# Values projected token by token and shifted by a DMA, in a hybrid of two attentions and an FFN

## The chip, the cores and the metric

The program runs on one core of a Trainium2 chip. Its engines are TensorE (PE), VectorE (DVE), ScalarE (ACT), GpSimd (POOL) and SyncE (SP, which only issues DMAs here). Each takes its instructions in the order in which they are written, and engines wait for each other through semaphores. The metric is the device time of one execution in microseconds, lower is better.

## The reference

Four layers with residual sums on x of 4 batches x 2048 tokens x 256 channels, float32: causal attention A, an FFN with token shift, attention B, and the FFN again. Each takes a layer norm of x.

```python
x = x + attn_a(layernorm(x), q_proj, k_proj, v_proj, o_proj)          # 16 heads of 16
x = x + ffn(layernorm(x), W_r, W_k, W_v, mu_r, mu_k)
x = x + attn_b(layernorm(x), W_k, W_v, W_c, leaky_key_beta, key_scale, v_coef, val_scale)
x = x + ffn(layernorm(x), ...)                                        # the same weights
```

The change lies in the keys and values of attention B:

```python
k = (x @ W_k.T)  # by head; then a decaying sum over earlier tokens
k = einsum('hij,bhjd->bhid', exp(-(i - j) * beta_h) for j <= i, k)
k = k / (norm(k) + 1e-10) * exp(min(10 * key_scale, KEY_SCALE_MAX))
v = (x @ W_v.T)
v_shift = concatenate([v[:, :, 1:], zeros])
v = (1 - v_coef) * v_shift + v_coef * v       # v_coef: one number per head
v = v / (norm(v) + 1e-10) * exp(10 * val_scale)
q = k[:, :, 1:]                               # queries are the keys one token on
```

Queries are the keys one token later, so the kernel keeps values one place back as well: at place n it mixes the value of token n-1 (times `v_coef`) and the value of token n (times `1 - v_coef`).

## The kernel before

There are eight attentions (A and B, each for four batches), and each has four groups of four heads: 32 instances. An instance is a row of 68 slots. In a slot PE computes the scores of a group of two 128x512 blocks (three slots ahead), ACT takes their exponential into `probs`, POOL masks the blocks on the diagonal (`mask`, the last five groups of each of the four query chunks), and PE multiplies earlier `probs` with `v_st`. The query chunks end with slots 4, 17, 38 and 67; after each, `take` on DVE transposes the sums out of PSUM (`o_blk`, which sets the semaphore `s_o`), divides them (`o_norm`), and for every second head group transposes them to `o_out`, which SP stores to memory. Two banks of PSUM (6 and 7) alternate between the query chunks; the one not in use serves all side work.

The side work is cut into jobs of one chunk of 512 tokens. P jobs normalize x and project queries, keys and values of attention A. M jobs project the attention's output (`o0`, `o1`), add it to x, normalize, turn `xn` (`t0`, `t1`), and run the FFN (`k`, `r`, `f`). MA jobs (16, four batches x four chunks) go on with attention B: normalize again, turn (`bt0`, `bt1`), project keys (`bk0`, `bk1`) and values (`bv0`, `bv1`). Keys run through a scan on DVE and a transposition in blocks (`k_blk`), POOL squares them (`buf_a`). Values are projected channel by channel into `vT` (copied by ACT), so that the shift by one token is a shift along the row; POOL weights them (`buf_u`), DVE mixes them, PE turns them to tokens (`vt0`, `vt1`, line 981), ACT copies them to `buf_v`, POOL squares them into `buf_k`. Then DVE sums both kinds of squares and computes the inverse lengths of keys and values in one row of operations on 128 columns (line 1389 on), gives `v_fac` to POOL and scales the keys.

The order is written out by hand: the tables `T_P`, `T_M`, `T_B` and `T_END` hold a slot offset for each step, and a step stands on its engine at the job's start plus this offset; in one slot the main work comes first, then the jobs in their order. M jobs start four slots before an instance (`FRONT`). Each side part waits with `free_bank` until the part before it in its bank is emptied and until the bank's query chunk has been taken:

```python
if part.before:
    pe.wait_ge(s_side[part.bank], part.before)
if part.seg > 0:
    pe.wait_ge(s_o, part.seg)
```

Three slots before each instance all engines read flags that tell whether a head needs its row maxima; DVE, SP and PE branch there. Four heads of the run are flagged.

Of the kernel before, what the change touches and what calls it, by code (L numbers as in the profile page):

```python
# [105 lines left out]
class Job:  # L106
# [4 lines left out]
    def __init__(self, kind, b, c, att, t0, off=None):  # L111
# [8 lines left out]
T_P0 = {"load": -10, "ln": 0, "t0": 6, "t1": 8, "u0": 14, "u1": 16, "u2": 18, "u3": 20, "v0": 22, "v1": 24, "n": 28,  # L120
# [3 lines left out]
T_M = {"load": -10, "o0": 0, "o1": 2, "ln": 3, "t0": 12, "t1": 14, "diff": 13, "shift": 16, "k0": 18, "k1": 20, "r0": 26,  # L124
       "r1": 28, "f0": 30, "f1": 32, "out": 34}
# [6 lines left out]
PE_PARTS["MA"] = PE_PARTS["MB"] + ("bt0", "bt1", "bk0", "bk1", "bv0", "bv1", "vt0", "vt1")  # L132
# [3 lines left out]
def job_list():  # L136
# [15 lines left out]
    jobs += [Job("MB", 3, c, 7, start(7, 3) + (16, 37, 58, 82)[c], T_END) for c in range(NCH)]  # L152
# [84 lines left out]
JOB = {(j.kind, j.b, j.c): j for j in JOBS}  # L237

# [17 lines left out]
def hybrid_kernel(nc, t, out):  # L256
    with ExitStack() as ctx:
# [31 lines left out]
        vT = sb("vT", [P, KT, CH + 1])  # L289
# [117 lines left out]
        def _(sp):  # L407
# [68 lines left out]
            def load_o(j):  # L476
# [91 lines left out]
            def main(slot):  # L568
# [6 lines left out]
                if 0 <= n < NI and i in LAST_OF and n % 2:  # L575
# [970 lines left out]
```

## Time and profile before

| | |
|---|---|
| Median of 3 runs (lowest, highest) | 3010.07 us (3009.12, 3013.25) |
| The profiled execution | 3010.78 us, span 3009.1 us |
| PE busy | 2862.4 us, 95% |
| ACT busy | 2232.7 us, 74% |
| DVE busy | 1472.8 us, 49% |
| POOL busy | 817.1 us, 27% |
| Mean granted clock of PE | 0.976 |

"Busy" is the time in which an engine executes something; waiting and issuing are not in it. Each row of a timeline is one or several like instructions, with the idle time of the engine just before it in brackets and what ended it. PE's records of a float32 matmul come in pairs, so 32 records are 16 matmuls.

### The profile page before, as it was taken

The numbers are of one execution on the slowest core, as the hardware profiler recorded it, in microseconds if no ns is written. First come the engines' busy times: TensorE is split into PE (matmuls) and PEld (weight loads), VectorE is DVE, ScalarE is ACT, GpSimd is POOL, SyncE is SP. The second block draws the span as 40 slices with busy tenths as digits, with TensorE's granted clock in tenths as the row PEclk, the third lists the DMA queues.
The fourth block names the chain that finished last, engine by engine and source line by source line (L and its number), as shares of the span: only waits on it lengthen the run. The fifth ranks groups of instructions, "written<-read, shape, count | busy, mean of one in ns | idle before, by whom it ended". The sixth has DMA issues, their size and how long they took to land.

```text
span 3009.1 us, 99722 instructions
## 1 busy us (share of the span) xinstructions
PE 2862.4 (95%) x42984; PEld 1302.0 (43%) x42984; DVE 1472.8 (49%) x3579; ACT 2232.7 (74%) x2487; POOL 817.1 (27%) x1246
## 2 busy tenths in 40 slices
PE   6999999999999899998999999999999989999897
PEld 3444444444444344444444444444444434444343
DVE  5322346565556654445344434555665656523544
ACT  2799978787787478784788878778787856788472
POOL 4222223332323222221222222232333322322111
PEclk9999999999999899998999999999999999999898
DMA  5322312222222123222322223222222221222111
GB/s 136 106 83 81 95 53 78 70 73 67 81 71 60 52 67 103 81 76 67 95 81 74 82 89 94 64 78 68 63 75 71 73 66 52 72 72 85 41 62 41
DMA packets 229828, 225.34 MB, mean 75 GB/s; under 512 B 33221, under 2 KB 212933, under 8 KB 229320
## 3 DMA queue, kind: packets, MB, share of 16 engines
q1 hardware_dynamic: 228504, 217.47, 25.3%
q8 instruction: 356, 5.83, 0.8%
q14 instruction: 152, 1.25, 0.1%
q10 hardware_dynamic: 816, 0.79, 0.1%
HBM read 146.80 MB, written 71.32 MB: 72 GB/s over the span
## 4 chain that ended last, share of the span: by engine, by line
PE 72%; DVE 16%; issue 6%; ACT 4%; POOL 1%; SPq 0%; DVEq 0%; DMA 0%; ACTq 0%
PE ps L872 46%; PE ps L1103 23%; ACT probs L828 4%; DVE pmax L1434 3%; PE ps L884 3%; DVE xn L1198 2%; DVE nw_y L1180 1%; DVE nw_u L1178 1%; DVE ln_st L1186 1%; DVE nw_u L1176 1%; DVE x_buf L1315 1%; DVE o_blk L1493 1%; DVE k_blk L1413 1%; DVE nw_v L1389 1%; POOL buf_k L703 0%
## 5 line engine op out<-in xcount | busy, mean ns | idle before, releaser
L828 ACT ACTIVATE probs<-ps 128x1024 f32<-128x1024 f32 x2176 | 2083.1, 1059 | 477.7 <-PE ps L872 474.5
L872 PE MATMUL ps<-q_st,k_st 99*32 99x512 bf16 (+3 forms) x20480 | 1237.4, 349 | 5.0 <-issue 2.4
L1103 PE MATMUL ps<-probs,v_st 128*17 128x512 f32 (+3 forms) x10240 | 1160.7, 532 | 22.4 <-POOL probs L731 13.1
L872 PEld LDWEIGHTS ps<-q_st,k_st 99*32 99x32 bf16 x20480 | 567.0, 96 | 775.7 <-issue 449.6
L731 POOL TENSOR_SCALAR_AFFINE_SELECT probs<-probs 128x256 f32<-128x256 f32 (+1 forms) x896 | 433.4, 501 | 1138.7 <-ACT probs L828 1120.1
L1103 PEld LDWEIGHTS ps<-probs,v_st 128*17 128x17 f32 x10240 | 291.9, 98 | 272.2 <-issue 59.1
L872 PE MATMUL ps<-xT,wT 128*32 128x512 f32 x2048 | 242.6, 594 | 0.0
L1493 DVE STREAM_TRANSPOSE o_blk<-ps 128x512 f32<-128x512 f32 x128 | 91.0, 711 | 269.2 <-PE ps L1103 268.9
L657 POOL TENSOR_TENSOR parts<-rest,parts 128x512 bf16<-128x512 f32 x96 | 120.9, 1260 | 316.7 <-DVE parts L1221 316.7
L1348 DVE SCALAR_TENSOR_TENSOR buf_v<-buf_v,ps 128x512 f32<-128x512 f32 x64 | 44.0, 687 | 272.9 <-PE ps L872 272.9
L1315 DVE TENSOR_TENSOR x_buf<-x_buf,ps 128x512 f32<-128x512 f32 x64 | 43.8, 684 | 217.6 <-PE ps L872 207.2
L872 PE MATMUL ps<-wT,o_in 128*32 128x256 f32 x2048 | 124.3, 380 | 14.5 <-issue 14.5
L872 PE MATMUL ps<-buf_k,wT 128*32 128x512 f32 x1024 | 124.7, 609 | 8.2 <-DVE buf_k L1335 8.0
L872 PEld LDWEIGHTS ps<-xT,wT 128*32 128x32 f32 x2048 | 65.1, 109 | 139.8 <-issue 136.1
L872 PE MATMUL ps<-wT,buf_u 128*32 128x256 f32 x2048 | 121.9, 379 | 1.6 <-issue 1.6
L872 PE MATMUL ps<-wT,buf_a 128*32 128x256 f32 x2048 | 121.6, 379 | 0.6 <-issue 0.5
L884 PE MATMUL ps<-ident,xn 128*128 128x128 f32 x512 | 85.8, 293 | 34.7 <-DVE xn L1198 24.5
L792 ACT ACTIVATE buf_u<-ps 128x512 f32<-128x512 f32 x64 | 38.2, 597 | 99.9 <-PE ps L872 99.9
L884 PEld LDWEIGHTS ps<-ident,xn 128*128 128x128 f32 x512 | 55.8, 145 | 125.1 <-DVE xn L1198 63.1
L1216 DVE TENSOR_TENSOR rest<-ps,parts 128x512 f32<-128x512 f32 x64 | 44.1, 690 | 133.5 <-ACT parts L778 133.5
L681 POOL TENSOR_TENSOR buf_a<-xf 128x512 f32<-128x512 f32 x32 | 33.2, 1037 | 270.3 <-DVE xf L1204 255.5
L1198 DVE TENSOR_SCALAR xn<-x_buf,ln_mv,nw_y 128x256 f32<-128x256 f32 x256 | 99.3, 450 | 2.3
(140 smaller groups left out, 2148.9 us busy)
## 6 DMA issues: line engine op xcount, KB each, us to landing
part_a<-parts SPq DMA_DIRECT2D x192, 128.0 KB
x_buf<-in_L_attn_a_X SPq DMA_DIRECT2D x32, 512.0 KB, 4.6
q_st<-part_a SPq DMA_DIRECT2D x128, 128.0 KB
o_chan<-o_out SPq DMA_DIRECT2D x64, 256.0 KB, 2.4
o_in<-o_chan SPq DMA_DIRECT2D x64, 256.0 KB, 4.6
q_st<-part_b SPq DMA_DIRECT2D x128, 128.0 KB
k_st<-part_a SPq DMA_DIRECT2D x64, 192.0 KB, 2.9
part_b<-parts SPq DMA_DIRECT2D x96, 128.0 KB
```

What stands on the lines that cost most here:

```text
L657: pool.tensor_tensor(parts[:, u % NPARTS, 2, :], rest[:, u % 2, :], parts[:, u % NPARTS, 1, :], ALU.subtract).then_inc(s_low, 1)
L731: last = pool.affine_select(out=o, in_=o, compare_op=ALU.is_ge, fill=0.0, base=0, pattern=[[0, o.shape[1]], [1, P]], channel_multiplier=-1)
L828: nc.scalar.activation(probs[:, g % NP_BUF, :], ps[:, bk:bk + 2, :].rearrange("p a n -> p (a n)"), ACT.Exp, scale=SCALE[ATT[g // (NHG * NG ...
L872: last = pe.matmul(o[c:c + 32], kt[:, c:c + 32], q, **how)
L884: last = pe.transpose(ps[:, part.bank, tb * P:(tb + 1) * P], src[:, tb, kt * P:(kt + 1) * P], ident[:, :])
L1103: last = pe.matmul(ps[32 * j:32 * j + VW, bank, q0:q0 + w], v_st[:, k % 2, kb, hg * HG + j, :], p, start=(kb == 0), stop=(kb >= TB * qc), ...
L1198: last = nc.vector.tensor_scalar(xn[:, tb, :], x[:, tb, :], ln_mv[:, tb, 0:1], nw_y[:, tb:tb + 1], ALU.subtract, ALU.mult)
L1216: nc.vector.tensor_tensor(left, src, high, ALU.subtract).then_inc(s_side[part.bank], 1)
L1315: nc.vector.tensor_tensor(half(x, i), half(x, i), ps[:, part.bank, :], ALU.add).then_inc(s_side[part.bank], 1)
L1348: nc.vector.scalar_tensor_tensor(half(gate, i), half(gate, i), 1.0, ps[:, part.bank, :], ALU.add, ALU.mult).then_inc(s_side[part.bank], 1)
L1434: nc.vector.tensor_reduce(pmax[:, 1 if b0 else 0, qb:qb + 1], src, AX_X, ALU.max).then_inc(s_mx["used"], 1)
L1493: nc.vector.transpose(o_blk[:, sg % 2, :], ps[:, 6 + sg % 2, :]).then_inc(s_o, 1)
```

## The change

Values of attention B are now projected token by token (`project_tokens`) straight into the layout in which they are used; ACT copies them to `v_raw`. SP shifts them by one token with three DMAs within SBUF: 127 partitions of `v_raw` to the next partition of `v_before` (the memory of `buf_k`), the last partition to the first of the next block, and the very last token to `v_edge` for the next chunk; POOL places the edge. POOL weights `v_raw` with `v_rest`, DVE mixes per head with factors that are spread over the elements of a head (four operations for two), POOL squares. `vt0` and `vt1` are gone. The lengths are computed in two rows of operations on 64 columns, of keys (`klen`) and of values (`vlen`), at two places.

The tables move further steps: `o0` and `o1` of all M jobs stand two slots earlier, with their loads; the normalization of the first batch's chunks stands five slots earlier, with a wait on PE's turn of the chunk before; at the start x of the second chunk is loaded only when the first has landed. The last four jobs start 6 to 13 slots earlier, and the last output chunk's second half goes from DVE into `o_in` without a store and a load.

```diff
-T_P0 = {"load": -10, "ln": 0, "t0": 6, "t1": 8, ...}
+T_P0 = {"load": -16, "ln": -5, "t0": 6, "t1": 8, ...}
-T_M = {"load": -10, "o0": 0, "o1": 2, "ln": 3, "t0": 12, ...}
-T_B = {"lnb": 32, "bt0": 40, "bt1": 46, "bk0": 48, "bk1": 50, "bv0": 52, "bv1": 54, "w": 55, "u": 57, "vt0": 59, "vt1": 61,
-       "len": 63, "keys": 69, "split": 91, "vb": 70, "low": 94, "store": 98}
+T_M = {"load": -12, "o0": -2, "o1": 0, "ln": 3, "t0": 12, ...}
+T_B = {"lnb": 32, "bt0": 40, "bt1": 46, "bk0": 48, "bk1": 50, "bv0": 52, "bv1": 54, "w": 55, "vsh": 56, "u": 61, "vsq": 63,
+       "klen": 55, "vlen": 73, "split": 91, "vb": 82, "low": 94, "store": 98}
+T_LAST = {**T_END, "o_load": -4}
...
-    jobs += [Job("MB", 3, c, 7, start(7, 3) + (16, 37, 58, 82)[c], T_END) for c in range(NCH)]
+    jobs += [Job("MB", 3, c, 7, start(7, 3) + (10, 24, 45, 69)[c], {**T_LAST, "load": -4} if c == 2 else T_LAST) for c in range(NCH)]
...  SP
+                yield j.t0 + j.off["vsh"]
+                for i in range(2):
+                    sp.wait_ge(*emptied(j.at[f"bv{i}"]))
+                sp.dma_start(v_before[1:P], v_raw[0:P - 1]).then_inc(s_vsh, 16)
+                sp.dma_start(v_before[0:1, 1:TB, :], v_raw[P - 1:P, 0:TB - 1, :]).then_inc(s_vsh, 16)
+                sp.wait_ge(s_edge, j.at["ma"] + 1)
+                sp.dma_start(v_edge[:, :], v_raw[P - 1:P, TB - 1, :]).then_inc(s_vsh, 16)
...
-            for c in range(2):
-                load_x(JOB["P", 0, c])
+            load_x(JOB["P", 0, 0])
+            sp.wait_ge(s_x[0], 16)
+            load_x(JOB["P", 0, 1])
...  POOL
-                    pool.tensor_scalar(buf_u[:, m, :], vT[:, m, 1:CH + 1], v_rest[:, m:m + 1], None,
+                    pool.tensor_tensor(by_head(half_of(buf_u, i)), by_head(half_of(v_raw, i)), per_head(v_rest),
                                        ALU.mult).then_inc(s_w1, 1)
...
+                    pool.wait_ge(s_u, 2 * n + i + 1)
+                    pool.tensor_tensor(half_of(buf_k, i), half_of(buf_v, i), half_of(buf_v, i), ALU.mult).then_inc(s_vsq, 1)
...  PE
+                        if j is LAST_JOB:
+                            pe.wait_ge(s_o_in, 32 * f + 16)
+                            pe.wait_ge(s_ot, len(ATT) * KT * NCH)
...
+                    if at == j.off[f"bv{i}"]:
+                        project_tokens(j.at[f"bv{i}"], BV, i, src)
...  DVE
+            def inverse_lengths(at):
+                step(nc.vector.tensor_scalar(nw_v[:, at], nw_v[:, at], 1.0e-30, None, ALU.max))
+                settle()
+                rsqrt(at)
+                step(nc.vector.tensor_tensor(nw_u[:, at], nw_v[:, at], nw_y[:, at], ALU.mult))
+                settle()
+                step(nc.vector.tensor_scalar(nw_u[:, at], nw_u[:, at], NORM_EPS, None, ALU.add))
+                settle()
+                step(nc.vector.reciprocal(nw_y[:, at], nw_u[:, at]))
+                settle()
...
+                yield j.t0 + j.off["u"]
+                dve.wait_ge(s_edge, n + 1)
+                dve.wait_ge(s_vsh, 48 * (n + 1))
+                for i in range(2):
+                    step(nc.vector.tensor_tensor(by_head(half_of(buf_v, i)), by_head(half_of(v_before, i)), per_head(v_coef),
+                                                 ALU.mult))
+                    settle()
+                    dve.wait_ge(s_w1, 2 * n + i + 1)
+                    nc.vector.tensor_tensor(half_of(buf_v, i), half_of(buf_v, i), half_of(buf_u, i), ALU.add).then_inc(s_u, 1)
+                yield j.t0 + j.off["vlen"]
                 dve.wait_ge(s_vsq, 2 * (j.at["ma"] + 1))
+                step(sums(buf_k, of_values))
+                settle()
+                inverse_lengths(of_values)
...
+                    if sg == NI * NCH - 1:
+                        dve.wait_ge(s_part, JOBS[-2].at["o1"].n + 1)
+                        dst = o_in[:, KT - 1, :]
```

DVE at the start of a new instance, before: after the normalization of the job that has just begun (`xn`) comes `take` of the new instance's first query chunk.

```order
L1178 SCALAR_TENSOR_TENSOR nw_u<-nw_u,nw_v 128x4
L1180 SCALAR_TENSOR_TENSOR nw_y<-nw_u,nw_y 128x4
L1198 TENSOR_SCALAR xn<-x_buf,ln_mv,nw_y 128x256 x4
L1493 STREAM_TRANSPOSE o_blk<-ps 128x512
L1496 TENSOR_SCALAR den<-o_blk 128x16
```

The same place of the changed kernel (nine more operations of the inverse root on 128x64 stand where rows are left out):

```order
L1236 TENSOR_SCALAR xn<-x_buf,ln_mv,nw_y 128x256 x4
L1208 TENSOR_REDUCE nw_v<-buf_k 128x64
L1211 TENSOR_SCALAR nw_v<-nw_v 128x64
L1195 TENSOR_SCALAR nw_y<-nw_v 128x64
L1197 TENSOR_SCALAR nw_y<-nw_y 128x64
...
L1214 TENSOR_TENSOR nw_u<-nw_v,nw_y 128x64
L1216 TENSOR_SCALAR nw_u<-nw_u 128x64
L1218 RECIPROCAL nw_y<-nw_u 128x64
L1443 TENSOR_TENSOR v_fac<-nw_y,v_scale 128x64
L1525 STREAM_TRANSPOSE o_blk<-ps 128x512
```

The lengths of the previous job's values have moved from before the change of instance to between `xn` and `o_blk`; this is so in all 16 jobs.

PE at the change of instance, before (`wT,o_in` are the parts `o0` and `o1`, `TENSOR_LOAD` and the branch read the flags):

```order
L1103 MATMUL ps<-probs,v_st 17x512 x4
L872 MATMUL ps<-wT,o_in 32x256 x16
L1142 TENSOR_LOAD flags_a
L1143 COMPARE_AND_BRANCH
L872 MATMUL ps<-q_st,k_st 32x512 x16
L1103 MATMUL ps<-probs,v_st 17x384 x4
L1103 MATMUL ps<-probs,v_st 17x128 x4
L872 MATMUL ps<-wT,o_in 32x256 x16
```

And in the changed kernel:

```order
L1127 MATMUL ps<-probs,v_st 17x512 x4
L901 MATMUL ps<-wT,o_in 32x256 x16
L901 MATMUL ps<-q_st,k_st 32x384 x4
L901 MATMUL ps<-q_st,k_st 32x128 x4
...
L901 MATMUL ps<-q_st,k_st 32x256 x16
L1127 MATMUL ps<-probs,v_st 17x512 x4
L901 MATMUL ps<-wT,o_in 32x256 x16
L1166 TENSOR_LOAD flags_a
L1167 COMPARE_AND_BRANCH
```

Both output projections now stand ahead of the branch.

SP in the last quarter of an MA job's instance, before, with the loads of the next job behind the keys:

```order
L511 DMA k_st<-part_a 48x4x512
L511 DMA k_st<-part_a 32x4x512
L511 DMA k_st<-part_a 16x4x512
L435 DMA x_buf<-in_L_attn_a_X 128x4x256
L483 DMA o_in<-o_chan 128x512 x2
```

And in the changed kernel:

```order
L539 DMA k_st<-part_a 16x4x512
L486 DMA buf_k<-v_raw 127x1024
L487 DMA buf_k<-v_raw 1x16x48
L489 DMA v_edge<-v_raw 1x16x16
L452 DMA x_buf<-in_L_attn_a_X 128x4x256
L511 DMA o_in<-o_chan 128x512 x2
```

The three DMAs of the shift stand ahead of the next job's loads.

## Rows read from the trace of the kernel before

**Rows 1.** The page's busy times: us (share of the span) xinstructions.

```profile
PE 2862.4 (95%) x42984; PEld 1302.0 (43%) x42984; DVE 1472.8 (49%) x3579; ACT 2232.7 (74%) x2487; POOL 817.1 (27%) x1246
```

**Rows 2.** Waits of PE: engine, line <- releaser: us in total, times, longest.

```profile
PE ps L1103 <- POOL probs L731: 13.1, 9, 2.5
...
PE ps L884 <- DVE o_blk L1493: 10.1, 14, 1.2
```

**Rows 3.** Groups of PE by form: busy us, mean ns | idle before.

```profile
L872 PE MATMUL ps<-xT,wT 128*32 128x512 f32 x2048 | 242.6, 594 | 0.0
...
L872 PE MATMUL ps<-wT,o_in 128*32 128x256 f32 x2048 | 124.3, 380 | 14.5 <-issue 14.5
...
L872 PE MATMUL ps<-wT,xT 128*32 128x256 f32 x1024 | 64.3, 391 | 0.5 <-DVE rest L1216 0.5
...
L981 PE MATMUL ps<-ident,buf_u 128*128 128x128 f32 x128 | 21.0, 287 | 0.0
```

**Rows 4.** Timeline, a change of head group: start, us, engine, [idle before <-releaser].

```profile
556.33 1.04 PE L872 MATMUL ps<-q_st,k_st 99*32 99x512 bf16 x16
...
558.63 0.67 DVE L1315 TENSOR_TENSOR x_buf<-x_buf,ps 128x512 f32<-128x512 f32 x1
...
559.40 1.93 PE L872 MATMUL ps<-wT,o_in 128*32 128x256 f32 x32 [1.17 <-issue]
...
561.13 0.65 PE L872 MATMUL ps<-q_st,k_st 99*32 99x384 bf16 x16
...
563.37 1.38 DVE L1413 TENSOR_TENSOR k_blk<-k_blk,nw_v 128x1024 f32<-128x1024 f32 x1 [3.28 <-issue]
...
565.58 1.05 PE L1103 MATMUL ps<-probs,v_st 128*17 128x512 f32 x8 [2.49 <-POOL probs L731]
```

**Rows 5.** Timeline, a change of head group without lengths of values.

```profile
1295.86 0.65 PE L1103 MATMUL ps<-probs,v_st 128*17 128x256 f32 x8
...
1297.15 0.70 DVE L1493 STREAM_TRANSPOSE o_blk<-ps 128x512 f32<-128x512 f32 x1
...
1299.48 0.34 DVE L1192 BATCH_NORM_AGGREGATE ln_mv<-ln_st 128x2 f32<-128x6 f32 x4
...
1303.53 0.71 DVE L1493 STREAM_TRANSPOSE o_blk<-ps 128x512 f32<-128x512 f32 x1
...
1304.43 0.66 PE L884 MATMUL ps<-ident,xn 128*128 128x128 f32 x4
```

**Rows 6.** Groups of DVE by form.

```profile
L1178 DVE SCALAR_TENSOR_TENSOR nw_u<-nw_u,nw_v 128x4 f32<-128x4 f32 x192 | 33.9, 176 | 6.6
...
L1389 DVE TENSOR_REDUCE nw_v<-buf_k 128x64 f32<-128x1024 f32 x16 | 19.5, 1220 | 76.7 <-POOL buf_k L703 76.7
...
L1178 DVE SCALAR_TENSOR_TENSOR nw_u<-nw_u,nw_v 128x128 f32<-128x128 f32 x48 | 18.6, 388 | 1.6
...
L1399 DVE RECIPROCAL nw_y<-nw_u 128x128 f32<-128x128 f32 x16 | 15.2, 953 | 0.6
```

**Rows 7.** Waits of all engines: DVE before the keys' scaling.

```profile
DVE k_blk L1413 <- issue: 22.1, 7, 3.3
```

**Rows 8.** Timeline of the tail, PE.

```profile
2957.04 2.59 PE L1103 MATMUL ps<-probs,v_st 128*17 128x384 f32 x24 [1.96 <-issue]
...
2966.02 6.05 PE L872 MATMUL ps<-buf_k,wT 128*32 128x512 f32 x32 [4.78 <-DVE buf_k L1335]
...
2975.35 1.90 PE L872 MATMUL ps<-wT,o_in 128*32 128x256 f32 x32
...
2991.79 5.12 PE L872 MATMUL ps<-buf_k,wT 128*32 128x512 f32 x32 [3.24 <-DVE buf_k L1335]
```

**Rows 9.** Windows: us, busy by engine, then the granted clock of PE.

```profile
742.03:745.44 3.41, 3.41 (x40) 1.75 (x36) 3.03 (x16) 1.94 (x2) 0.00 (x0) 0.50 0.19 70
```

**Rows 10.** Timeline of the head.

```profile
36.46 0.66 PE L884 MATMUL ps<-ident,xn 128*128 128x128 f32 x4 [2.60 <-DVE xn L1198]
```

**Rows 11.** DMA issues of the page: KB each, us to landing.

```profile
x_buf<-in_L_attn_a_X SPq DMA_DIRECT2D x32, 512.0 KB, 4.6
```

More of the change, by code:

```diff
@@ L481, in load_o @@
                 for m in range(KT):
+                    if j is LAST_JOB and m == KT - 1:
+                        continue
                     sp.wait_ge(s_o_out[j.c % 2], 16 * ((k * KT + m) * (NCH // 2) + j.c // 2 + 1))
@@ L678, in m_job @@
                 if any(i.kind == "MA" for i in earlier):
-                    pool.wait_ge(s_vfac, [i for i in earlier if i.kind == "MA"][-1].at["ma"] + 1)
+                    pool.wait_ge(s_ksum, [i for i in earlier if i.kind == "MA"][-1].at["ma"] + 1)
                 pool.wait_ge(*emptied(j.at["t0"]))
@@ L850, in params @@
                 for kt in range(KT):
-                    pe.matmul(ps[:, 0, 2 * kt:2 * kt + 2], sel_ch[:, kt * P:(kt + 1) * P], head_col[:, 0:2],
-                              start=True, stop=True)
+                    pe.matmul(ps[:, 0, kt:kt + 1], sel_ch[:, kt * P:(kt + 1) * P], head_col[:, 0:1], start=True, stop=True)
                 for i in range(4):
@@ L855, in params @@
                 pe.matmul(ps[:, 1, 0:H], ones_row[:, :], head_row[:, :], start=True, stop=True)
+                pe.matmul(ps[:, 1, H:2 * H], ones_row[:, :], coef_row[:, :], start=True, stop=True)
                 pe.matmul(ps[0:1, 2, 0:H], head_col[:, 2:3], ident[0:H, 0:H], start=True, stop=True).then_inc(s_hp_ps, 1)
@@ L966, in m_job @@
                         turn(j.at[f"bt{kt}"], xn, kt)
[L967 to L983 removed]
+                for i in range(2):
+                    if at in (j.off[f"bk{i}"], j.off[f"bv{i}"]):
+                        for kt in range(KT):
+                            pe.wait_ge(*emptied(j.at[f"bt{kt}"]))
+                    if at == j.off[f"bk{i}"]:
+                        project_channels(j.at[f"bk{i}"], BK, i, src)
+                    if at == j.off[f"bv{i}"]:
+                        project_tokens(j.at[f"bv{i}"], BV, i, src)
             def row_maxima(n, j):
@@ L1251, in p_job @@
             def p_job(j):
-                yield j.t0
+                yield j.t0 + j.off["ln"]
+                if j.b == 0 and j.c:
+                    dve.wait_ge(s_part, JOB["P", 0, j.c - 1].at["t1"].n + 1)
                 x_there(j)
@@ L1372, in m_job @@
                     nc.vector.transpose(k_blk[:, m, :], kT[:, m, :]).then_inc(s_kblk, 1)
-                yield j.t0 + j.off["u"]
-                for m in range(KT):
-                    dve.wait_ge(s_w1, 2 * j.at["ma"] + m + 1)
-                    nc.vector.scalar_tensor_tensor(buf_u[:, m, :], vT[:, m, 0:CH], v_coef[:, m:m + 1], buf_u[:, m, :],
-                                                   ALU.mult, ALU.add).then_inc(s_u, 1)
-                dve.wait_ge(s_u, 2 * (j.at["ma"] + 1))
-                if j.c < NCH - 1:
-                    nc.vector.tensor_copy(vT[:, :, 0:1], vT[:, :, CH:CH + 1]).then_inc(s_vlast, 1)
-                else:
-                    nc.vector.memset(vT[:, :, 0:1], 0.0).then_inc(s_vlast, 1)
@@ L1391, in m_job @@
-                settle()
-                step(nc.vector.tensor_scalar(nw_v[:, :], nw_v[:, :], 1.0e-30, None, ALU.max))
-                settle()
-                rsqrt(P)
-                step(nc.vector.tensor_tensor(nw_u[:, :], nw_v[:, :], nw_y[:, :], ALU.mult))
-                settle()
-                step(nc.vector.tensor_scalar(nw_u[:, :], nw_u[:, :], NORM_EPS, None, ALU.add))
-                settle()
-                step(nc.vector.reciprocal(nw_y[:, :], nw_u[:, :]))
-                settle()
```

134 lines of the change are left out of this document (67 added, 67 removed).

## The prediction

> **What bounds the kernel now.** I read the page's busy times first: PE is busy for 95% of the span, ACT and DVE for 74% and 49% [rows 1]. So time is what PE computes plus what PE stands idle, 147 us in all. Next PE's own waits, to see who makes it idle: at most of the head-group changes it waits a short time for DVE's `o_blk` and for POOL's masks [rows 2], and the second `o_in` projection of a job is preceded by idle time as well, 14.5 us over the run, labelled "issue" [rows 3]. The timeline at one such change shows that the label misleads. `x_buf` is added by DVE at 558.63, only after a long row of small operations on lengths, and the next `o_in` matmul starts 0.1 us after that add has ended: both use one bank of PSUM, so PE had waited for DVE. Then DVE stands 3.28 us at the branches on the flags, adds the second half, and PE's products with `v_st`, which need the same bank, start at 565.58 after 2.49 us [rows 4]. So DVE's order around a change of head group decides PE's idle time, and there the change must be weighed.
>
> **Transposes and projection.** 16 jobs (four batches by four chunks) give up 8 PE transposes each: the row with `buf_u` has 128, 21.0 us [rows 3]. Their values are projected token by token: 64 records of 256 columns in a job for 32 of 512. By the rows 64 x 62.8 ns = 4.02 us for 32 x 118.5 ns = 3.79 us; by the `o_in` row (60.7 ns) 3.88 us. That is +1.5 to +3.6 us in all, and I take +2.5. PE is the bound wherever this lies, so the sum is -18.5 us. ACT loses two copies in a job; it is not the bound.
>
> **The earlier `o_in` projections.** They move two slots forward, and the second one now stands ahead of the branch on PE, and its add ahead of the flag branches on DVE. DVE's small operations on keys are now done some ten slots before, on values after the change of group. So the waits of that timeline should go: 14.5 us before `o_in` [rows 3], and 10.1 and 13.1 us from the two wait rows [rows 2], 37.7 us; I take -37 (-34 to -41).
>
> **The chain of the values' lengths.** This is the step that speaks against the change. In the order of DVE it now stands behind the `xn` of the next job and directly ahead of the first `o_blk` of the new head group, in all 16 jobs. PE's first transposes of `xn` (slot 8) wait for that `o_blk`, because it empties their bank, and everything on PE queues behind them. The same place without lengths of values, where PE waits for nothing, gives the cover [rows 5]. PE's last products of the old group end at 1296.51, its transposes start at 1304.43: 7.92 us. DVE needs 2.33 us from its first `o_blk` to the normalization (0.71 less where the head group is even and `o_out` isn't written), 4.05 us to the second `o_blk`, and 0.74 us until that bank is free. With 0.1 us to start that is 7.2 us, so 0.7 us of cover. Now the chain: a sum of 1.22 us, 14 operations on 64 columns, a reciprocal and `v_fac`. No row has them at 64 columns. At 4 columns one takes 0.18 us, at 128 0.39 us [rows 6], each with 0.03 us to the next; the 128 figure includes operations beside a busy POOL, which is idle here between its masks, so I take 0.25 us with the gap. 1.22 + 3.5 + 0.55 (reciprocal, 0.95 at 128) + 0.35 = 5.7 us; the bounds are 4.7 us (all as at 4 columns) and 8.0 us (all as at 128). PE's stall is then 5.7 - 0.7 = 5.0 us, 4.3 us at even groups, 4.7 us on average. DVE also has to pass the flag branches first: seven times of 16 these cost it 3.3 us [rows 7]. After the second add and statistics (1.4 us) that is 4.7 us, and PE has 3.0 us of scores and products from there to the end of the group (556.33 to 558.23, and 1.1 us from 561.13), so DVE comes 1.7 us late in such a case, 0.8 us on average. 16 x 5.5 us = +88 us (+59 with the chain at 4.7 us and no branch time, +125 at 8.0 us).
>
> **TensorE's clock.** After an idle time of 4.78 us the next 32 records took 6.05 us, after 3.24 us 5.12 us [rows 8], for 3.79 us at full clock [rows 3]: 2.3 and 1.3 us lost, at the lower of its two levels (1.2 for 2.4 GHz). I take 1.8 us for each of 16 stalls, +29 us, less three stretches of 1.7 us that the present short waits bring (one is the row of 742.03 [rows 9]; the others are alike): +24 us. The row of 565.58 had 2.49 us of idle time before it and ran at its full speed (1.05 us for 8 records), so not every short wait costs the clock; at changes of the head group three of the six between 2.1 and 2.7 us did. The Trainium skill, "TensorE: Matmul & The Clock Gate", section "Part 1: The HAM clock gate", calls the throttled state the default, which activity releases. If the busy stretches on both sides are activity enough by that rule, a 5 us stall passes as the one of 2.49 us did, and the sum is the second rival's below; by the two waits of [rows 8] it does not pass, and I follow the rows.
>
> **The shift by DMA.** Its wait adds a risk on DVE: behind it stand the adds of `o_in`. No row shows a transfer within SBUF. The nearest are `x_buf` from memory, 512 KB in 4.6 us [rows 11], and I take 4 us (2.4 to 10). Issued in slot 52, it lands about when DVE has finished the keys' chain (some 8.5 us from slot 51); the mixing (four operations, 3.3 us) ends some 2 us before the first add is due. Cost 0; if the cover goes, each us more is 16 us in the sum. POOL's squares end just before its masks: 0 as well.
>
> **Head and tail.** At the start PE waits three times 2.6 us for `xn` of the next chunk [rows 10]; the normalization now stands ahead of the splits. DVE's own work in a chunk is some 13 us for PE's 12.6, so two thirds of it come back, 6 us. But the parameters, which DVE still awaits first, are now issued only after the first chunk has landed, which costs 1 to 2 us. Together -5 (-8 to +2). In the tail PE's products end at 2959.63, the last `o_in` parts stand behind work of the job before (8 transposes, 32 records of 512 and 64 of 256 columns: 1.3 + 3.8 + 3.9 = 9 us at the rates of [rows 3]), and the first starts at 2975.35 [rows 8]. Now the last half of `o` comes from DVE without memory, some 2.5 us after the products, and those 9 us are moved ahead of them, where PE pays them too. 2975.35 - 2959.63 - 2.5 - 9 = 4 us: -4 (-11 to +2, as the earlier jobs wait more closely for their `o_in`).
>
> **Sum.** -18.5 - 37 + 88 + 24 - 5 - 4 = +47.5 us against the profiled execution of 3010.78 us (span 3009.1 us, and 1.7 us around it), 0.7 us over the median of the three timed ones: 3058, and against the median 3057 us.
>
> **Rivals.** First, the other side: the `o_blk` is not late. If DVE passes normalization and chain within PE's 7.92 us, or PE reaches its transposes later than I think, the 88 and 24 us are gone: -18.5 - 37 - 5 - 4 = -64.5, 2946 us. For it speaks that DVE is busy only 49% of the span; against it that the cover is 0.7 us and the shortest chain is 4.7 us. It decides only from a chain under 0.7 us, or if another row of slots lies between.
> Second, the stalls come but the clock mostly stays: half of them pay 1.7 us, 14 - 5 = +9 in place of 24, 3043 us. For it the 2.49 us case; against it [rows 8].
> Third, the shift lands late, say after 10 us. Then the mixing ends 4 us after the adds are due, POOL's masks and PE behind them: 16 x 4 = +64, 3122 us. Against it: `x_buf` in 4.6 us.
> Fourth, balance: chain 4.7 us and no branch time (+59), clock +17, and the gains at their upper ends (-19.5, -41, -8, -11): -3.5, 3007 us.
> That the change doesn't do what it says I can exclude by the order: no transposes of `buf_u` are left, and three DMAs stand in each job.
>
> **How the numbers follow.** The likeliest case 0.62, its own range 3020 to 3100 (chain 4.7 to 7 us); clock stays 0.14; not late 0.12; late landing 0.07; balance 0.05. The range reaches from the balanced case to most of the high bound of the chain (88 becomes 125: 3094 and the clock above): 3005 to 3110, which leaves out 2946 and the late landing. What can be told from no change is 0.2%, 6 us. Faster by more: the 0.12 and half the balanced case, 0.15; the same 0.03; slower 0.82.
>
> **What would show it.** PE before its first transposes of `xn` in a new head group: idle 4 to 7 us, released by `o_blk`, 16 times. The chain on 64 columns between `xn` and `o_blk`: 5 to 6.5 us. No idle time before the second `o_in`. Half-clock stretches after those transposes. No PE row with `buf_u` transposes, and PE's busy time 18 us less but for the clock's part. The shift lands within 6 us. The forecast is wrong if `o_blk` is there before PE, or if the mixing waits for the DMA into the adds.

## The result and the profile after

The changed kernel takes 3423.3 us (median of 4 runs, 3421.4 to 3426.5) against 3009.8 us: a ratio of 1.1372, 95% interval 1.1353 to 1.1392. It is slower, as forecast, but by 413 us where 47 were forecast. The profiled execution took 3423.03 us, its span is 3421.3 us.

From the page after: busy times [rows 1], then the chain of work that ended last, by engine and by line.

```profile
PE 2913.5 (85%) x43370; PEld 1341.3 (39%) x43370; DVE 1548.4 (45%) x3833; ACT 2215.4 (65%) x2455; POOL 797.8 (23%) x1261
...
PE 63%; DVE 14%; SPq 8%; DMA 7%; issue 5%; ACT 2%; POOL 0%; DVEq 0%; ACTq 0%
PE ps L901 41%; PE ps L1127 19%; DMA o_in<-o_chan 6%; SPq L487 4%; PE ps L913 2%; DVE pmax L1466 2%; SPq L511 2%; DVE xn L1236 2%; ACT probs L857 2%; DVE nw_u L1200 1%; DVE nw_u L1202 1%; DVE o_blk L1525 1%; DVE nw_y L1204 1%; SPq L489 1%; SPq L539 1%
```

PE's busy time rose by 51 us and its idle time from 147 to 508 us. The reader is to see two names that had no part in the profile before: a DMA of `o_in`, and SP's own queue at L487, the second of the three DMAs of the shift. The groups of the page say who waited for what (busy, mean ns | idle before, releaser). The first is the group of `wT,o_in` in [rows 3], the second has the waits for `o_blk` of [rows 2], and the third is DVE's mixing:

```profile
L901 PE MATMUL ps<-wT,o_in 128*32 128x256 f32 x2048 | 153.9, 450 | 310.0 <-DMA o_in<-o_chan 308.0
...
L913 PE MATMUL ps<-ident,xn 128*128 128x128 f32 x512 | 96.0, 318 | 128.4 <-DVE o_blk L1525 108.3
...
L1433 DVE TENSOR_TENSOR buf_v<-buf_k,v_coef 128x512 f32<-128x512 f32 x32 | 22.0, 688 | 359.8 <-DMA v_edge<-v_raw 359.8
```

In each of the 16 jobs PE stands 18.4 to 19.6 us ahead of the first projection of `o_in`, and DVE 22.5 us on average for the shift. The timeline of one job, SP's issues (how long each took) and the two that waited:

```profile
450.56 0.69 SPq L486 DMA_DIRECT2D buf_k<-v_raw  x1
...
451.30 8.25 SPq L487 DMA_DIRECT2D buf_k<-v_raw  x1
...
459.59 0.85 SPq L489 DMA_DIRECT2D v_edge<-v_raw  x1
460.49 0.59 SPq L452 DMA_DIRECT2D x_buf<-in_L_attn_a_X  x1
461.18 6.13 SPq L511 DMA_DIRECT2D o_in<-o_chan  x2
467.35 4.44 SPq L539 DMA_DIRECT2D k_st<-part_a  x3
475.48 0.69 DVE L1433 TENSOR_TENSOR buf_v<-buf_k,v_coef 128x512 f32<-128x512 f32 x1 [22.27 <-DMA v_edge<-v_raw]
...
477.69 3.64 PE L901 MATMUL ps<-wT,o_in 128*32 128x256 f32 x32 [18.56 <-DMA o_in<-o_chan]
```

The shift's first DMA was issued at 450.56 and the data were there at 475.48. The trace has 127 packets of 4096 bytes in this time, one for each row of L486, from 452.00 to 474.49, with a mean of 181 ns: 127 x 181 ns = 23.0 us of packet time in 22.5 us, hardly more than one packet under way at any moment. I read that as one of the 16 DMA engines carrying them all; rows118 and rows124 test it. The packets of `o_in` bear it out: of the 256 of its two DMAs, issued from 461.18 on, 240 had started by 469.83, and the other 16, one in 16, ran from 475.89 to 477.09, behind the shift. The first projection then also ran at the lower level of the clock (the granted clock was 0.50 from 462.24 to 482.72): 3.64 us for the 32 records that took 1.93 us before [rows 4].

The stalls that the prediction spoke of are there as well: the 108.3 us above. DVE's operations around one of them, the last before `o_blk` being those of the lengths, and PE behind:

```profile
493.44 1.39 DVE L1236 TENSOR_SCALAR xn<-x_buf,ln_mv,nw_y 128x256 f32<-128x256 f32 x4
494.74 1.22 DVE L1208 TENSOR_REDUCE nw_v<-buf_k 128x64 f32<-128x1024 f32 x1
...
500.08 0.22 DVE L1443 TENSOR_TENSOR v_fac<-nw_y,v_scale 128x64 f32<-128x64 f32 x1
500.23 0.71 DVE L1525 STREAM_TRANSPOSE o_blk<-ps 128x512 f32<-128x512 f32 x1
...
501.08 1.09 PE L913 MATMUL ps<-ident,xn 128*128 128x128 f32 x4 [4.91 <-DVE o_blk L1525]
```

From 494.74 to 500.23 the chain takes 5.5 us, and PE waits 4.91.

### The profile page after: what moved, and what is told of

It reads as the page before. It is cut to its first block, busy times and chain, and to the rows that moved or that the text cites. A ratio compares the mean times of both kernels' runs of the same rounds, so it can differ in the third digit from the quotient of the medians.

```text
span 3421.3 us, 100825 instructions
## 1 busy us (share of the span) xinstructions
PE 2913.5 (85%) x43370; PEld 1341.3 (39%) x43370; DVE 1548.4 (45%) x3833; ACT 2215.4 (65%) x2455; POOL 797.8 (23%) x1261
## 4 chain that ended last, share of the span: by engine, by line
PE 63%; DVE 14%; SPq 8%; DMA 7%; issue 5%; ACT 2%; POOL 0%; DVEq 0%; ACTq 0%
PE ps L901 41%; PE ps L1127 19%; DMA o_in<-o_chan 6%; SPq L487 4%; PE ps L913 2%; DVE pmax L1466 2%; SPq L511 2%; DVE xn L1236 2%; ACT probs L857 2%; DVE nw_u L1200 1%; DVE nw_u L1202 1%; DVE o_blk L1525 1%; DVE nw_y L1204 1%; SPq L489 1%; SPq L539 1%
## 5 line engine op out<-in xcount | busy, mean ns | idle before, releaser
L901 PE MATMUL ps<-q_st,k_st 99*32 99x512 bf16 (+3 forms) x20480 | 1258.5, 355 | 2.6 <-DVE flags_a L1340 2.3
L1127 PE MATMUL ps<-probs,v_st 128*17 128x512 f32 (+3 forms) x10240 | 1173.3, 536 | 2.8 <-issue 1.1
L901 PEld LDWEIGHTS ps<-q_st,k_st 99*32 99x32 bf16 x20480 | 577.2, 98 | 762.3 <-issue 437.2
L765 POOL TENSOR_SCALAR_AFFINE_SELECT probs<-probs 128x256 f32<-128x256 f32 (+1 forms) x896 | 419.8, 486 | 1124.8 <-ACT probs L857 1114.1
L901 PE MATMUL ps<-wT,o_in 128*32 128x256 f32 x2048 | 153.9, 450 | 310.0 <-DMA o_in<-o_chan 308.0
L901 PEld LDWEIGHTS ps<-wT,o_in 128*32 128x32 f32 x2048 | 76.4, 126 | 398.1 <-DMA o_in<-o_chan 324.6
L913 PE MATMUL ps<-ident,xn 128*128 128x128 f32 x512 | 96.0, 318 | 128.4 <-DVE o_blk L1525 108.3
L1433 DVE TENSOR_TENSOR buf_v<-buf_k,v_coef 128x512 f32<-128x512 f32 x32 | 22.0, 688 | 359.8 <-DMA v_edge<-v_raw 359.8
L901 PE MATMUL ps<-xT,wT 128*32 128x512 f32 x1536 | 181.2, 594 | 2.4 <-DVE n_max L1315 2.4
L737 POOL TENSOR_TENSOR buf_k<-buf_v 128x512 f32<-128x512 f32 x32 | 39.3, 1230 | 436.6 <-DVE buf_v L1437 436.6
L901 PE MATMUL ps<-wT,xT 128*32 128x256 f32 x2048 | 123.6, 380 | 0.2 <-DVE rest L1254 0.2
```

The source lines that it names most:

```text
L765: last = pool.affine_select(out=o, in_=o, compare_op=ALU.is_ge, fill=0.0, base=0, pattern=[[0, o.shape[1]], [1, P]], channel_multiplier=-1)
L901: last = pe.matmul(o[c:c + 32], kt[:, c:c + 32], q, **how)
L913: last = pe.transpose(ps[:, part.bank, tb * P:(tb + 1) * P], src[:, tb, kt * P:(kt + 1) * P], ident[:, :])
L1127: last = pe.matmul(ps[32 * j:32 * j + VW, bank, q0:q0 + w], v_st[:, k % 2, kb, hg * HG + j, :], p, start=(kb == 0), stop=(kb >= TB * qc), ...
```

## The experiments

Every ratio is to the kernel before, timed beside it on the same chip; a kernel's name is that of its experiment. Times in us of kernels from different groups of runs are set side by side below; the kernel before moved by 1.3 us between these groups. Line numbers move by one or two where lines were added.

**rows112**, the first edit, only cuts the shift's large DMA in two, with the semaphore counts raised from 48 to 64 for the fourth DMA.

```diff
-sp.dma_start(v_before[1:P], v_raw[0:P - 1]).then_inc(s_vsh, 16)
+sp.dma_start(v_before[1:113], v_raw[0:112]).then_inc(s_vsh, 16)
+sp.dma_start(v_before[113:P], v_raw[112:P - 1]).then_inc(s_vsh, 16)
```

> The changed kernel with the shift of partitions 0-126 to 1-127 (L486, 127 rows of 4 KB) cut in two DMAs, 112 rows and 15 rows; nothing else. Theory A (one DMA engine): the trace of the changed kernel has 127 packets of 4096 B from 452.00 to 474.49 us, 181 ns each, which is 23.0 us end to end, so all of them went through one of the 16 DMA engines; that engine's share of the next job's o_in waits behind them. With 112 = 16 x 7 rows the packets spread: the shift lands within about 3 us, the 16 PE waits of 18.4 to 19.6 us at ps<-wT,o_in go (-300 us), the L487 issue falls from 8.4 to 0.7 us, DVE's 359.8 us of waits for v_edge go: about 3423 - 300 = 3123 us (3090 to 3150), the 16 stalls of about 5.5 us at slot 8 stay. Theory B (the one-partition DMAs L487 and L489 are what is slow, or SP's issue): nothing changes, 3423 +- 10.

Measured: 3118.8 us, ratio 1.0354 (1.0337 to 1.0372). Theory A's forecast holds and theory B falls: 304.5 us of the 413 are this one DMA. SP's issues in the same job, then the waits (us in total, times, longest):

```profile
453.08 0.64 SPq L486 DMA_DIRECT2D buf_k<-v_raw  x1
453.76 0.89 SPq L487 DMA_DIRECT2D buf_k<-v_raw  x1
454.70 1.72 SPq L488 DMA_DIRECT2D buf_k<-v_raw  x1
456.46 0.59 SPq L490 DMA_DIRECT2D v_edge<-v_raw  x1
457.10 0.59 SPq L452 DMA_DIRECT2D x_buf<-in_L_attn_a_X  x1
```

```profile
PE ps L914 <- DVE o_blk L1526: 108.8, 25, 7.5
PE ps L902 <- DMA o_in<-o_chan: 34.9, 19, 3.3
```

The wait for `o_in` fell from 308.0 to 34.9 us and PE's busy time from 2913.5 to 2885.3: 301 us together, for 297 of span. The wait for `o_blk` is untouched.

**rows118** and **rows124** cut the same DMA in 118 and 9, and in 124 and 3 rows, to see what decides how many engines share it.

```diff
-sp.dma_start(v_before[1:P], v_raw[0:P - 1]).then_inc(s_vsh, 16)
+sp.dma_start(v_before[1:119], v_raw[0:118]).then_inc(s_vsh, 16)    # rows124: 1:125, 0:124
+sp.dma_start(v_before[119:P], v_raw[118:P - 1]).then_inc(s_vsh, 16)  # rows124: 125:P, 124:P - 1
```

> The changed kernel with the shift of partitions 0-126 cut in DMAs of 118 and 9 rows in place of 112 and 15. In the changed kernel 127 rows (a prime number) took 127 x 181 ns = 23 us, as if through one DMA engine; in rows112 the shift landed 3.8 to 4.8 us after its first issue. Theory A1 (the number of engines that share a DMA is the largest divisor of its outer count that is not above 16): 118 = 2 x 59 goes through 2 engines, 59 x 0.18 = 10.7 us, 9 rows through 9; DVE's wait for v_edge is about 7 + 3 = 10 us each, and PE's wait for o_in about 7 us in place of 19: 3119 + 16 x (5 to 8) = 3200 to 3250 us. Theory A2 (only a multiple of 16 is spread, anything else goes through one engine): 118 x 0.18 = 21.3 us, time as the changed kernel, 3400 to 3425 (and 15 rows in rows112 cost 15 x 0.18 = 2.7 us). Theory A3 (rows are dealt out in turn and only the count of 127 was bad): as rows112, 3119.

> The changed kernel with the shift cut in 124 and 3 rows: a third point of the dose. 127 rows took 22.5 us (one engine), 118 rows 12.6 us (59 packets of 4 KB in each of two engines, 0.21 us each), 112 rows 2.4 to 3.5. If the count of engines is the largest divisor up to 16, 124 = 4 x 31 goes through 4 engines: 31 x 0.22 = 6.8 us from first to last packet (6 to 8), DVE's wait for v_edge about 6 to 7 us each, and 3119 + 16 x 3 to 4 = 3165 to 3185 us. If instead an even count gives two engines, 62 x 0.21 = 13 us and 3270 us, as with 118 rows.

Measured: rows118 3269.5 us, ratio 1.0855 (1.0837 to 1.0873); rows124, one run, 3223.9 us. The 4 KB packets of the shift in the four kernels, counted from the traces (time from the start of the first to the end of the last, median of 16 jobs; how many were under way at once, mean over the second job):

```
rows of the DMAs   largest divisor to 16   first to last   under way
127                1                       22.6 us         1.0
118 and 9          2 and 9                 12.9 us         2.2
124 and 3          4 and 3                  9.4 us         3.2
112 and 15         16 and 15                2.4 us        14.0
```

DVE's wait for the shift in rows118, then in rows124, and PE's for `o_in` in rows118:

```profile
DVE buf_v L1434 <- DMA v_edge<-v_raw: 203.4, 16, 13.9
...
PE ps L902 <- DMA o_in<-o_chan: 153.0, 19, 10.3
```

```profile
DVE buf_v L1434 <- DMA v_edge<-v_raw: 162.2, 16, 11.3
```

The order of the four is theory A1's, and the number under way is close to the divisor each time; A2 and A3 fall. The Trainium skill, "DMA: Bandwidth & Descriptors", section "Why a DMA increments its semaphore by 16 and not by 1", says just this: the number of engines is the largest one up to 16 that divides the slowest dimension that isn't 1 of both sides, and it names 127 partitions as a case of one engine. The traces agree, with 1.0, 2.2, 3.2 and 14.0 packets under way. What missed: rows118 cost 150.6 us more than rows112 and not 80 to 130. PE's waits for `o_in` rose by 118.1 us (34.9 to 153.0) and its busy time by 26.2 us (2885.3 to 2911.5) with the same instructions, and the expectation had no such second part. rows124 cost 105 us and not 46 to 66: its 124 rows took 9.4 us where 31 x 0.22 = 6.8 were expected, on an average of 3.2 packets under way and not 4. Why fewer than four were under way stays open.

**loads_first** puts the loads of `x_buf` and `o_in` ahead of the slow DMA on SP.

```diff
-T_M = {"load": -12, "o0": -2, "o1": 0, ...}
+T_M = {"load": -13, "o0": -2, "o1": 0, ...}
```

> The changed kernel with the next job's x_buf and o_in loads one slot earlier (load at -13 in T_M), so that on SP they stand ahead of the three shift DMAs; the shift itself unchanged. Theory A: o_in lands before the slow DMA takes its engine, so the 16 PE waits for o_in (308 us) go, but the shift still takes 22 us and DVE's wait for v_edge (359.8 us) stays; keys' loads (k_st) behind the shift on SP come about 9 us late. 3110 to 3180 us if the u step's lateness is covered. Theory B (SP's issue of 8.4 us alone is what delays o_in): the same gain here, but none in the run with 112 rows. Rival C: DVE's wait of 23 us, queued ahead of pmax and o_blk work, holds PE as well: then the time stays above 3250.

Measured: 3436.2 us, ratio 1.1407 (1.1377 to 1.1436). Theory A's number for this run is too low by more than 250 us, and rival C is right. The timeline of PE, POOL and DVE there:

```profile
476.74 0.69 DVE L1433 TENSOR_TENSOR buf_v<-buf_k,v_coef 128x512 f32<-128x512 f32 x1 [23.33 <-DMA v_edge<-v_raw]
...
478.24 1.42 POOL L737 TENSOR_TENSOR buf_k<-buf_v 128x512 f32<-128x512 f32 x1 [27.51 <-DVE buf_v L1437]
...
481.28 2.80 POOL L765 TENSOR_SCALAR_AFFINE_SELECT probs<-probs 128x256 f32<-128x256 f32 x7
...
482.10 1.91 PE L1127 MATMUL ps<-probs,v_st 128*17 128x512 f32 x8 [20.17 <-POOL probs L765]
```

`o_in` is there in time, but the late shift holds DVE's mixing, that holds POOL's squares, POOL's masks stand behind the squares, and PE's products behind the masks. So the shift's lateness had two ways to PE, and closing one opened the other: 16 waits of 18.4 to 19.6 us for `o_in` in the changed kernel, 16 of 17.7 to 20.4 us for POOL's masks here.

**vlen77** and **rows112_vlen77** move the lengths of the values behind the `o_blk` that PE's first transposes wait for, in the changed kernel and in rows112.

```diff
-       "klen": 55, "vlen": 73, "split": 91, "vb": 82,
+       "klen": 55, "vlen": 77, "split": 91, "vb": 82,
```

> The changed kernel with vlen at 77 for 73, so that DVE's chain of the values' lengths stands behind the o_blk of slot 8 and not ahead of it. My theory: the 16 stalls of 4.5 to 7.4 us at ps<-xn (108.3 us of waits for o_blk in all, 25 times) go: 3423 - 80 to 100 = 3325 to 3345 us, with the waits for o_in unchanged at 16 x 19. Rival: the stall moves to the chain's next user (k_blk, the first turns of xf) or to v_st's loads and less than half is won: above 3380.

> Both edits: the shift in 112 and 15 rows, and vlen at 77. If the two costs are separate and add, 3123 - 88 = about 3035 us by the waits alone; the prediction's own terms without its term for the lengths give 2969 (2940 to 3010). Rival: the clock gives nothing back and DVE's later chain moves the stall: above 3060, slower than before (3010).

Measured: 3413.3 us, ratio 1.1329 (1.1310 to 1.1348), and 3110.2 us, ratio 1.0324 (1.0302 to 1.0347). Both times the rival: 10 and 8.6 us won, not 80 to 100. The order of DVE and PE in rows112_vlen77:

```profile
474.45 0.71 DVE L1526 STREAM_TRANSPOSE o_blk<-ps 128x512 f32<-128x512 f32 x1
...
475.81 0.66 PE L914 MATMUL ps<-ident,xn 128*128 128x128 f32 x4
...
482.11 0.23 DVE L1444 TENSOR_TENSOR v_fac<-nw_y,v_scale 128x64 f32<-128x64 f32 x1
482.25 0.69 DVE L1243 COPY xf<-ps 128x512 f32<-128x512 f32 x1
...
483.04 1.08 PE L914 MATMUL ps<-ident,xn 128*128 128x128 f32 x4 [4.73 <-issue]
```

PE's first transposes start without a wait here, and its second ones stand 4.73 us. They start 0.1 us after DVE's copy of the first ones has ended, and that copy stands behind the chain. The stall moved by one step, in all 16 jobs (3.2 to 5.3 us), under the label "issue".

**split_len** cuts the lengths in two, in rows112: the sum right behind the squares, the chain behind `xf`, where DVE had stood idle for 6.2 us in rows112_vlen77. The mixing and the squares move one slot forward with it, and the step of `v_st` seven slots back.

```diff
-yield j.t0 + j.off["vlen"]
+yield j.t0 + j.off["vsum"]
 dve.wait_ge(s_vsq, 2 * (j.at["ma"] + 1))
 step(sums(buf_k, of_values))
+yield j.t0 + j.off["vlen"]
...
-"vsh": 56, "u": 61, "vsq": 63, "klen": 55, "vlen": 73, "split": 91, "vb": 82,
+"vsh": 56, "u": 60, "vsq": 62, "klen": 55, "vsum": 65, "vlen": 85, "split": 91, "vb": 89,
```

> rows112 with the values' lengths cut in two: the sum over buf_k (1.2 us) right behind the squares (65, with u at 60 and the squares at 62), the chain of small instructions (4.7 us) at 85, in the gap of 6.2 us that DVE has there ahead of o_blk (490.16 to 496.32 in rows112_vlen77), and v_st's step at 89. In rows112 the 14 stalls at ps<-xn of 4.6 to 7.5 us are 84 us, and each is followed by 6.83 us at the half clock in the clock's record; at vlen 77 the stalls only moved to the second turns (4.2 to 5.3 us at ps<-xn behind DVE's copy of xf). Theory: both are the same 5 us of DVE between xn and xf; with the chain behind xf they go: 3119 - 84 - 14 x (2 to 3) of clock = 2990 to 3010 us. Rival: the chain delays buf_a/buf_k or v_st and PE waits there: above 3060.

Measured: 2994.5 us, ratio 0.9938 (0.9922 to 0.9955), 0.6% faster than the kernel before. PE before its first transposes in the same job (no idle time is left there), and the group over the whole run:

```profile
477.42 0.66 PE L914 MATMUL ps<-ident,xn 128*128 128x128 f32 x4
```

```profile
L914 PE MATMUL ps<-ident,xn 128*128 128x128 f32 x512 | 86.0, 293 | 46.3 <-DVE o_blk L1527 25.9 <-DVE xn L1237 19.5 <-issue 0.9
```

Against rows112, 124.3 us went: 82.9 us of waits for `o_blk` (108.8 to 25.9) and 42.1 us of PE's busy time (2885.3 to 2843.2) with the same instructions, which is the clock: its record has 271.9 us at the lower level in rows112 and 151.5 us in split_len. In rows112 the stall of 4.91 us that ended at 484.06 reached into this window at the lower level, which began 1.3 us before PE started again (us, busy by engine, granted clock; DMA share, GB/s):

```profile
482.74:489.57 6.83, 5.51 (x32) 2.20 (x32) 3.28 (x8) 1.94 (x2) 3.14 (x3) 0.50 0.10 38
```

**split_len_load13** adds the edit of loads_first to split_len.

> split_len with the next job's loads one slot earlier (-13), ahead of the shift on SP. rows112 still has 9 waits of 1.5 to 2.7 us for o_in; with the shift fast the earlier load should take them away: 15 to 25 us below split_len, 2970 to 2995 us. Rival (the loads ahead delay the shift by about 1.5 us and DVE's u step with it, or the clock's dips don't depend on these waits): the same as split_len within 5 us.

Measured: 2967.3 us, ratio 0.9858 (0.9841 to 0.9874), 27 us less. The same edit that gained nothing while the shift was late now takes the waits for `o_in` from 30.0 to 8.3 us, and PE's busy time from 2843.2 to 2834.4.

**before_tm**, **before_o_mid**, **rows112_o_later**, **best_o_later** and **best_o_mid** test the step of the earlier `o_in` projections in three surroundings. Each changes only the numbers of `T_M`.

```diff
 T_M = {"load": ..., "o0": ..., "o1": ...,
 # kernel before:     -10,  0, 2    before_tm:    -12, -2, 0    before_o_mid: -11, -1, 1
 # rows112:           -12, -2, 0    rows112_o_later: -10,  0, 2
 # split_len_load13:  -13, -2, 0    best_o_later: -13,  0, 2    best_o_mid:   -13, -1, 1
```

> The kernel before with one part of the change alone: the attention's output projected two slots earlier in the M jobs and its loads with it (load -12, o0 -2, o1 0). The prediction gave this part -37 us (the waits of PV for POOL's masks and x_buf, and for o_blk at slot 8). Theory: 2970 to 2985 us. Rival: the waits only move, 3005 to 3015.

> rows112 (3119 us) with the M jobs' loads and projections of o_in where they stood before (load -10, o0 0, o1 2). The prediction's term: these two slots are worth 37 us, so 3156. Rival 1: the stall of PE's first turns behind v_fac (108.8 us of waits for o_blk) hides most of it, since that chain stands later than either place: 3119 + 0 to 10. Rival 2 (as in the kernel before, where the step cost 35): 3085.

> split_len_load13 (2967 us) with the attention's output projection back where it stood in the kernel before: o0 at 0 and o1 at 2 for -2 and 0, the loads left at -13. In the kernel before this part alone cost +35 us (new waits of 2.31 us at ps<-wT,o_in), where the prediction had given it -37. Theory 1 (the step is worth its -37 only in company, where the turns of the values no longer stand on PE between the projections and slot 68): 2967 + 25 to 40 = 2990 to 3005 us. Theory 2 (what the step does is the same here as in the kernel before, it costs): 2930 to 2955. Theory 3 (nothing either way): 2962 to 2972.

> split_len_load13 with o0 at -1 and o1 at 1. split_len_load13 has 16 PE gaps of 1.1 to 2.25 us at ps<-xn behind DVE's o_blk, 25.2 us in all. If the step's place is a steady trade (later o0 moves x_buf, xn and the stall later, earlier ones collide with PV), this stands between split_len_load13 and best_o_later; if there is an optimum between, 2950 to 2960.

> The kernel before with the projections one slot earlier (load -11, o0 -1, o1 1), where two slots earlier cost +35 us by 16 new waits of 2.31 us at ps<-wT,o_in and 1.8 to 2.6 us at PV or xn in the same places. Theory (o0 at -2 meets a bank or a load of its own that -1 does not, and -1 takes the waits of PV and o_blk away as in best_o_mid, 30 us better than -2 and 37 better than 0 there): 2980 to 2995 us. Rival (in the kernel before the projections stand behind the turns of the values whatever their slot): 3010 to 3030.

```
                        o0 at 0     at -1       at -2
kernel before           3009.6      3006.2      3045.7
rows112                 3102.9      -           3118.8
split_len_load13        2974.1      2936.9      2967.3
```

before_tm has a ratio of 1.0114 (1.0097 to 1.0131), before_o_mid 0.9986 (0.9976 to 0.9995), rows112_o_later 1.0304 (1.0287 to 1.0321), best_o_later 0.9874 (0.9857 to 0.9892) and best_o_mid 0.9754 (0.9737 to 0.9770). The rows of before_tm show why two slots cost in the old surroundings:

```profile
471.23 0.95 DVE L1399 RECIPROCAL nw_y<-nw_u 128x128 f32<-128x128 f32 x1
...
472.72 0.67 DVE L1315 TENSOR_TENSOR x_buf<-x_buf,ps 128x512 f32<-128x512 f32 x1
...
473.50 1.72 PE L872 MATMUL ps<-wT,o_in 128*32 128x256 f32 x28 [2.31 <-issue]
```

The first add of `x_buf` waits behind the old chain of lengths on DVE, and the second projection waits for that add: 2.31 us in 14 jobs and 1.28 us in two. In the change that chain no longer stands there, but the loads come late. Between rows112_o_later and rows112 the waits for `o_in` rise from 9.3 to 34.9 us and those for `o_blk` from 94.8 to 108.8, against 24.6 us of waits for POOL's masks that go. In best_o_mid both are small:

```profile
PE ps L902 <- DMA o_in<-o_chan: 8.8, 3, 3.6
...
PE ps L914 <- DVE o_blk L1527: 4.1, 7, 1.1
```

One slot earlier is worth 37 us here, two slots 7, so the gain that I had seen exists, at another place and only once DVE's chain and the loads are out of the way. In the kernel before one slot is worth 3 us. My expectations fared badly. best_o_later has the sign of the first theory, but with 7 us and not 25 to 40 it lies 2 us from the range of the third, that nothing happens. before_tm is above both ranges, and rows112_o_later has the sign of its second rival at less than half of its size. before_o_mid lies between its two ranges, nearer to the rival, and best_o_mid came out 13 us below the range for an optimum between.

**best_old_tail** and **o_mid_old_tail** take back the starts of the last four MB jobs, and nothing else of the tail.

```diff
-... start(7, 3) + (10, 24, 45, 69)[c] ...
+... start(7, 3) + (16, 37, 58, 82)[c] ...
```

> split_len_load13 with the starts of the last four MB jobs back at 16, 37, 58 and 82 slots for 10, 24, 45 and 69; the last o_in half straight from DVE stays. The prediction gave the tail -4 us; from the last PV of the boundary before it to the end the traces show 269.6 us before and 272.4 us in split_len_load13, with three waits for o_in of 1.8 to 3.5 us in the latter. Theory (the prediction's: earlier starts pay): 2967 + 4 to 8. Rival (the earlier starts run into their own loads, and the tail lost 2.8 us by the change): 2967 - 3.

> best_o_mid (2937 us) with the starts of the last four MB jobs of the kernel before (16, 37, 58, 82). In split_len_load13 this took 5.6 us off, within the interval. If the tail's change costs as the traces say (three waits for o_in, 8.8 us): 2929 to 2934. If nothing: 2937.

Measured: 2961.7 us, ratio 0.9836 (0.9820 to 0.9853), 5.6 us less than split_len_load13, with intervals that overlap; and 2926.2 us, ratio 0.9721 (0.9705 to 0.9737), 10.7 us less than best_o_mid. The three waits for `o_in` (8.8 us) are gone from the latter, against 4.9 us more of waits for `buf_k`, and PE's busy time fell from 2833.9 to 2826.6, so the earlier starts cost time. What the last half straight from DVE is worth was not tried alone. o_mid_old_tail is the fastest kernel of the study, 2.8% under the kernel before. Its busy times:

```profile
PE 2826.6 (97%) x43370; PEld 1303.5 (45%) x43370; DVE 1584.9 (54%) x3833; ACT 2220.8 (76%) x2455; POOL 803.2 (27%) x1261
```

## Why the prediction was wrong in size

The step that failed is "The shift by DMA", in its own words: "No row shows a transfer within SBUF. The nearest are `x_buf` from memory, 512 KB in 4.6 us, and I take 4 us (2.4 to 10) ... Cost 0". It took 23 us, and the cost was 304.5 us by rows112, where the sum had put nothing. I carried over the rate of a DMA with 128 rows to one with 127. The row of `x_buf` [rows 11] is a transfer spread over many engines: in the trace before, 11 to 13 of its packets are under way at once, for the shift's 1.0. The size of a transfer didn't tell, its outer count did. The third rival had one of the two ways (the mixing late, POOL's masks and PE behind it), with a landing after 10 us as its end and a chance of 0.07. It did not have the other, by which the slow DMA delays the loads queued behind it on the same DMA engine, and that is the wait that PE shows in the changed kernel.

By terms, in us, each measured as named. The measurements stand in different surroundings, so that their sum comes near the whole is a check only in the rough:

```
term                              forecast   measured
transposes and projection         -18.5      -23     groups of PE, below
earlier o_in projections          -37        +16     rows112 against rows112_o_later
chain of lengths, with its clock  +88 +24    +124    rows112 against split_len
shift by DMA                       0         +304.5  the changed kernel against rows112
head                              -5         -6      trace, below
tail                              -4         +6, +11  its earlier starts alone, the two kernels with the old ones
sum                               +47.5      +421 to +426   (the change: +413.5)
```

**Transposes and projection.** Right. The groups after: 2048 records of `wT,xT` for 1024, 1536 of `xT,wT` for 2048, none of `buf_u`.

```profile
L901 PE MATMUL ps<-xT,wT 128*32 128x512 f32 x1536 | 181.2, 594 | 2.4 <-DVE n_max L1315 2.4
...
L901 PE MATMUL ps<-wT,xT 128*32 128x256 f32 x2048 | 123.6, 380 | 0.2 <-DVE rest L1254 0.2
```

Against [rows 3]: +59.3 - 61.4 - 21.0 = -23.1 us. The projection alone came to -2.1 us for +2.5, so that part had the wrong sign, at a size that didn't matter.

**The earlier projections.** Wrong in sign. The waits of [rows 4] did go (in rows112 0.7 us are left for POOL's masks), but I had not asked what the earlier step would itself wait for: its loads, two slots earlier on SP behind the shift, and DVE.

**The chain of the lengths.** Right in mechanism and place: 16 stalls of 4.5 to 7.4 us, released by `o_blk`, behind a chain of 5.5 us (5.7 forecast; the forecast's own parts add up to 5.6). The stalls are 94.3 us together, and 82.9 us of waits went with split_len, for 88. In the size there is some luck: seven of the stalls are 6.6 to 7.4 us and nine 4.5 to 5.1, but the seven aren't the jobs in which DVE stood 3 us at its branches before [rows 7], and in the one that ended at 615.70 DVE had waited 3.32 us for PE's products and for no branch. So the 0.8 us that I gave to the branches isn't shown, and what lengthens the seven stays open.

**The clock.** The direction was right, the size too small: 42 us for 24. I followed [rows 8] and not the 2.49 us case, and in that the traces agree: none of the 16 stalls of the changed kernel passed. Each has a stretch at the lower level that began before PE started again, 6.83 us long in 14 of them and 10.24 us in two. The second rival falls. A further 28 us of PE's busy time went with the slow shift (2913.5 to 2885.3 in rows112), which the forecast of the clock had no term for. That is why PE's busy time rose by 51 us where 18 less, but for the clock, were forecast; in split_len it is 19.2 us under the kernel before.

**Head.** Right. The last products of the first head group end at 161.0 us for 167.7 before, 161.5 in rows112: 6 to 7 us won for 5.

**Tail.** Wrong in sign. I had named the closer waits for `o_in` as a bound, and they were the outcome. The tail of the changed kernel itself was not tried alone; both measurements stand in the repaired kernels.

## What to carry to other kernels

Before a DMA is priced by its bytes, look at its outer count: a copy shifted by one row has 127, and with that a single DMA engine; cut it so that the large part divides by 16. A late transfer reaches the bound engine by every queue that stands behind it, so taking away one such wait shows nothing until the transfer itself is fast: mend the cause before tuning the order around it. When an operation is moved on a crowded engine, look for the next idle stretch there and for who waits behind it at each place in between, since a chain that is moved a little only hands its stall to the next consumer.

## What the runs showed of the hardware that I had not expected

The 127 packets, 520,192 bytes, went in 22.6 us with one under way: 23 GB/s, at best 156 ns for 4096 bytes. While it was at it, the issue of the next small DMA on SP took 8.25 us (median 8.4 over the 16 jobs), for a median of 0.7 in rows112 and 0.8 in rows118; in two of the jobs L487 took 0.64 and 0.91 us and L489 8.3 to 8.4. With 118 rows (two packets under way) this did not occur, and with 124 rows the same DMA took 2.0 us. What SP waits for there the runs don't show.
